# An adaLN block on one core: projections and attention rewritten in front of unchanged experts

## The reference

```
mod = silu(c) @ wmod                            # sa, ca, ga, sb, cb, gb
h = layernorm(x) * (1 + ca) + sa
q, k, v = h @ wq, h @ wk, h @ wv                # 32 query heads, 8 key heads, head width 8
att = softmax(causal(q k^T / sqrt(8)));  y = att @ v @ wo
x = x + ga * y
h = layernorm(x) * (1 + cb) + sb
w = top4_of_2_best_groups(softmax(h @ gate_w))  # 16 experts
x = x + gb * (sum_e w_e * swiglu_e(h) + shared(h))
```

## Time and profile before

| | us |
|---|---|
| median of three runs | 796.46 (795.24 to 807.66) |
| the profiled execution, and its span | 799.05, 797.3 |
| PE, DVE, ACT, POOL busy | 647.6, 456.4, 313.6, 356.1 |
| mean granted TensorE clock | 0.919 of full speed |

### The profile page before, as it was taken

How to read it: one execution, slowest core, us unless ns; L and a number is a source line. 1 busy time by engine, 2 the same in 40 slices (tenths; PEclk the granted TensorE clock), 3 DMA queues, 4 the chain that set the end, 5 groups by cost and what they waited for, 6 DMA issues and landing times.

```text
span 797.3 us, 12982 instructions
## 1 busy us (share of the span) xinstructions
PE 647.6 (81%) x3412; PEld 371.7 (47%) x3412; DVE 456.4 (57%) x751; ACT 313.6 (39%) x673; POOL 356.1 (45%) x440
## 2 busy tenths in 40 slices
PE   1599048999889998999877899992899999999940
PEld 1266023444335444434421555651567777777730
DVE  7576249858786867786728368972133333333317
ACT  1043002757565755575565433320233333333310
POOL 9322302443434352435241145776255666556640
PEclk9999678999999999999995889996899999999985
DMA  6047840315231423232010299656366666666658
GB/s 218 0 143 225 257 145 3 78 30 138 65 99 48 109 79 79 63 94 70 28 29 27 66 370 305 213 190 191 77 104 103 110 109 110 105 103 111 109 74 289
DMA packets 114137, 95.02 MB, mean 119 GB/s; under 512 B 47686, under 2 KB 106022, under 8 KB 114086
## 3 DMA queue, kind: packets, MB, share of 16 engines
q1 hardware_dynamic: 97462, 73.00, 31.8%
q0 software_dynamic: 14448, 19.31, 14.7%
q10 hardware_dynamic: 2176, 2.10, 0.8%
HBM read 47.66 MB, written 44.22 MB: 115 GB/s over the span
## 4 chain that ended last, share of the span: by engine, by line
PE 41%; DVE 11%; DMA 9%; issue 9%; POOL 9%; ACT 5%; SPq 3%; POOLq 0%; DVEq 0%; ACTq 0%
PE bank L980 9%; PE bank L795 7%; PE bank L998 7%; POOL x_rows L1201 6%; DVE negm L1237 5%; PE bank L785 4%; DMA y_sum<-arena 4%; ACT arena L1041 4%; PE bank L767 3%; PE bank L876 3%; DMA arena<-x_rows 3%; PE bank L968 2%; PE bank L813 2%; DVE arena L549 2%; PE bank L989 2%
## 5 line engine op out<-in xcount | busy, mean ns | idle before, releaser
L1041 ACT ACTIVATE arena<-bank 128x512 f32<-128x512 f32 x320 | 176.3, 599 | 117.0 <-PE bank L785 113.2
L1237 DVE TENSOR_REDUCE negm<-bank 128x2 f32<-128x1024 f32 (+3 forms) x176 | 190.8, 1117 | 36.7 <-PE bank L771 35.8
L1208 POOL DMA_INDIRECT y_sum<-arena x79 | 123.0, 1556 | 94.2 <-DVE arena L1455 89.9
L1147 POOL TENSOR_SCALAR_AFFINE_SELECT arena<-arena 128x512 f32<-128x512 f32 x128 | 81.7, 652 | 158.9 <-ACT arena L1041 155.1
L767 PE MATMUL bank<-arena 96*128 96x512 bf16 (+3 forms) x512 | 115.7, 307 | 35.8 <-DVE credits L1223 27.9
L785 PE MATMUL bank<-arena 96*128 96x512 bf16 x320 | 118.7, 399 | 15.8 <-ACT arena L1041 11.2
L980 PE MATMUL bank<-arena 128*128 x316 | 108.8, 467 | 0.3 <-issue 0.3
L771 PE MATMUL bank<-mask_qk,ident_bf 128*128 128x128 bf16 (+2 forms) x352 | 87.8, 250 | 0.0
L795 PE MATMUL bank<-arena 128*32 128x512 f32 x640 | 79.7, 627 | 5.1 <-POOL arena L1147 5.1
L1201 POOL DMA_INDIRECT x_rows<-arena,slots x64 | 63.3, 989 | 45.1 <-DVE slots L1370 26.2
L1448 DVE TENSOR_TENSOR arena<-bank,arena 128x176 f32<-128x176 f32 x79 | 27.0, 341 | 97.4 <-ACT arena L1119 97.4
(11 more groups left out here) (162 smaller groups left out, 750.5 us busy)
## 6 DMA issues: line engine op xcount, KB each, us to landing
arena<-x_rows SPq DMA_DIRECT2D x79, 136.5 KB, 2.5
q_parts<-arena SPq DMA_DIRECT2D x24, 384.0 KB, 3.9
arena<-q_parts SPq DMA_DIRECT2D x32, 288.0 KB
arena<-up_t SPq DMA_DIRECT2D x2, 2816.0 KB, 18.4
arena<-k_parts SPq DMA_DIRECT2D x16, 288.0 KB
y_parts<-arena SPq DMA_DIRECT2D x64, 64.0 KB
arena<-y_parts SPq DMA_DIRECT2D x16, 256.0 KB, 3.2
arena<-y_sum SPq DMA_DIRECT2D x8, 512.0 KB, 6.9
```

The source lines that it names most:

```text
L1041: nc.scalar.activation(pool[:, q % 2, g * QT + kt, :], bank[:, buf, :], ACT.Exp, scale=SCALE).then_inc(s["st_free"], 1)
L1147: nc.gpsimd.affine_select(out=block_, in_=block_, compare_op=ALU.is_ge, fill=0.0, base=0, pattern=[[0, REP], [1, P]], channel_multiplier=- ...
L1208: gp.indirect_dma_start(y_sum[t % 2], bass.IndirectOffsetOnAxis(ap=xt[t % XT][:, D:D + 1].bitcast(U32), axis=0), yo[t % YO], None, compute ...
L1237: nc.vector.tensor_reduce(to, view, AX.X, ALU.max, negate=True).then_inc(s["s_free"], 1)
```

## The change

The experts' code stays. In front of it:

- q parts are stored once (768 KB a batch), k parts too; each half's `Q` and `K` (one `K` now, rows 72 to 74 ones) are loaded whole, in three pieces each, into one of three buffers, two halves ahead.
- V is filled after the first norm, Q not at all, and 32 partitions of each K. Two norms are turned before the first projection, `hT` has two buffers, and q's banks alternate.
- The gates are made once, four batches as four rows, in the middle of the first maxima; SP writes them to memory and loads them broadcast.
- Probabilities stand in 4 slots of one group (4 tiles of one key tile). The diagonal group of a block comes first. PE weighs one group for each group of four exponentials, two groups behind; the eviction of a block comes inside a later group (`LEAVE`).
- The totals leave as one row a head. DVE inverts them as 128 x 64 at group 5; SP stores the inverse and loads it broadcast; the product comes at group 8. The last half inverts as before.
- The halves are unrolled, without loops and the registers of their waits. Statistics of the second norm, shared weights and the zero fills of the experts move ahead.

```diff
-KR = 96
+KR = PR + PARTS
...
+WEIGH = {n: (1, n + 8) if n < 2 else (0, n - 2) for n in range(NG)}
+LEAVE = {1: (1, 3), 2: (0, 0), 4: (0, 1), 7: (0, 2)}
+SLOTS = 4
+QBUF = 3
...
-        pool = take(2, 4 * GH, T)
-        Q = [take(QT, HH, P, dt=BF16) for s in range(2)]
-        K = [take(GH, T, dt=BF16) for s in range(2)]
-        K0 = [take(GH, T, dt=BF16) for s in range(2)]
-        Vc = [take(QT, GH, 32) for s in range(2)]
+        probs = take(SLOTS, GH, T)
+        Q = [take(HH, T, dt=BF16) for i in range(QBUF)]
+        K = [take(GH, T, dt=BF16) for i in (2, 0, 1)]
+        K = [K[1], K[2], K[0]]
...
-                nc.gpsimd.memset(V, 1.0).then_inc(s["v_ones"], 1)
-                for h in range(2):
-                    nc.gpsimd.memset(Q[h][:, :, :, :], 0.0)
-                    nc.gpsimd.memset(K[h][:, :, :], 1.0)
-                    last = nc.gpsimd.memset(K0[h][:, :, :], 0.0)
-                last.then_inc(s["cleared_q"], 1)
...
+                gp.wait_ge(s["xn_ready"], 1)
+                nc.gpsimd.memset(V, 1.0).then_inc(s["v_ones"], 1)
+                gp.wait_ge(s["v_ones"], 1)
+                for i in range(QBUF):
+                    nc.gpsimd.memset(K[i][64:96, :, :], 1.0).then_inc(s["k_ones"], 1)
+                    gp.wait_ge(s["k_ones"], i + 1)
+                low(0)
...
-                    for h in range(2):
-                        for j in range(PARTS):
-                            mine = parts[i][:, h, j, :].unsqueeze(1).to_broadcast([P, PARTS, T])
-                            sp.dma_start(q_parts[b, h, j].rearrange("n d h t -> (d h) n t"), mine).then_inc(q_out[i], 16)
-                        for n in range(PARTS):
-                            sp.dma_start(k_parts[b, h, n].rearrange("j d g t -> (d g) j t"),
-                                         parts[i][32 * h:32 * h + 32, 2, :, :]).then_inc(q_out[i], 16)
...
+                def store_parts(b):
+                    i = b % 2
+                    sp.wait_ge(s["low_done"], b + 1)
+                    sp.dma_start(q_parts[b].rearrange("h j d (n t) -> (d n) (h j) t", n=HH),
+                                 parts[i][:, 0:2, :, :].rearrange("p h j t -> p (h j) t")).then_inc(q_out[i], 16)
+                    sp.dma_start(k_parts[b].rearrange("j h d (g t) -> (h d g) j t", g=GH),
+                                 parts[i][0:64, 2, :, :]).then_inc(q_out[i], 16)
+                def load_half(u):
+                    b, h, i = u // 2, u % 2, u % QBUF
+                    for n in range(PARTS):
+                        rows_ = slice(PARTS * HD * n, PARTS * HD * n + PARTS * HD)
+                        sp.dma_start(Q[i][rows_, :, :].rearrange("p n t -> p (n t)"),
+                                     q_parts[b, h].rearrange("j d m -> (j d) m")).then_inc(q_in[i], 16)
+                        sp.dma_start(K[i][rows_, :, :].rearrange("p g t -> p (g t)"),
+                                     k_parts[b, n, h].unsqueeze(0).to_broadcast([PARTS, HD, GH * T])).then_inc(k_in[i], 16)
...
+                def send_values(u):
+                    h = u % 2
+                    sp.wait_ge(s["o_free"], QT * u + QT)
+                    above(sp, y_in[h], 32 * (u // 2))
                     for g in range(GH):
-                        for k in range(2):
-                            sp.dma_start(y_parts[h, k, g].rearrange("r d t -> d r t"),
-                                         O[h][32 * g + HD * k:32 * g + HD * k + HD, :, :]).then_inc(y_out[h], 16)
...
+                def fetch_values(u):
+                    h = u % 2
+                    sp.wait_ge(y_out[h], 128 * (u // 2 + 1))
...
+                    sp.dma_start(totals, y_totals[h].rearrange("n (a t) -> (n a) t", a=P // (GH * REP))).then_inc(t_in[h], 16)
+                    sp.dma_start(Yp[0][:, :], y_values[h].rearrange("g r d t -> (g r d) t")).then_inc(y_in[h], 16)
+                def spread_inverse(u):
+                    h = u % 2
+                    sp.wait_ge(s["inverted"], u + 1)
+                    sp.dma_start(y_inverse[h].rearrange("n (a t) -> (n a) t", a=P // (GH * REP)), inverse
+                                 ).then_inc(i_out[h], 16)
+                    sp.wait_ge(i_out[h], 16 * (u // 2 + 1))
+                    sp.dma_start(Yp[1][:, :], y_inverse[h].unsqueeze(1).to_broadcast([GH * REP, HD, T])).then_inc(y_in[h], 16)
...
+                store_parts(0)
+                store_parts(1)
+                sp.wait_ge(q_out[0], 32)
+                sp.wait_ge(s["k_ones"], QBUF)
+                load_half(0)
+                load_half(1)
+                store_parts(2)
+                store_parts(3)
+                sp.wait_ge(q_out[1], 32)
+                load_half(2)
+                sp.wait_ge(s["gate_rows"], 1)
+                sp.dma_start(mod_rows, row_mod[0:B, :, :].rearrange("p m d -> p (m d)")).then_inc(s["gate_out"], 16)
+                sp.wait_ge(s["gate_out"], 16)
...
+                for u in range(HALVES):
+                    if u > 0 and u + 2 < HALVES:
+                        sp.wait_ge(s["st_ready"], E_TOT * u)
...
+                        load_half(u + 2)
+                    put_negm(u, QT - 1)
+                    if u > 0:
+                        send_values(u - 1)
+                    if u + 1 < HALVES:
+                        put_negm(u + 1, 0)
+                    if u > 0:
+                        fetch_values(u - 1)
+                    if u + 1 < HALVES:
+                        put_negm(u + 1, 1)
+                    if u > 0:
+                        spread_inverse(u - 1)
+                    if u + 1 < HALVES:
+                        put_negm(u + 1, 2)
...
+                def gate_rows():
+                    pe.wait_ge(s["wg_in"], 16)
+                    for k in range(2):
+                        for c in range(DC):
+                            last = nc.tensor.matmul(bank[0:B, 6 + k, :], sc_sb[:, c, :],
+                                                    wmod_sb[:, c, GA * P + 512 * k:GA * P + 512 * k + 512],
+                                                    start=(c == 0), stop=(c == DC - 1))
+                    last.then_inc(s["gate_mm"], 1)
...
-                def weigh_values(b, h, q):
-                    u = 2 * b + h
-                    pe.wait_ge(s["p_ready"], 16 * u + 4 * q + 4)
-                    pe.wait_ge(s["o_free"], 4 * u + q + 1)
-                    for kt in range(q + 1):
-                        for g in range(GH):
-                            last = nc.tensor.matmul(bank[32 * g:32 * g + 32, OBANK, :], Vc[h][:, kt, g, :],
-                                                    pool[:, q % 2, g * QT + kt, :], start=(kt == 0), stop=(kt == q),
-                                                    skip_group_check=True)
+                def weigh_values(u, n):
+                    b, h, (q, kt) = u // 2, u % 2, GROUPS[n]
+                    pe.wait_ge(s["st_free"], E_TOT * u + GH * n + GH)
+                    if kt == q:
+                        pe.wait_ge(s["p_ready"], GH * (QT * u + q) + GH)
+                        above(pe, s["o_free"], QT * u + q)
+                    for g in range(GH):
+                        last = nc.tensor.matmul(bank[32 * g:32 * g + 32, OBANK, :], V[:, b * QT + kt, h * GH + g, :],
+                                                probs[:, (NG * u + n) % SLOTS, g, :], start=(kt == q),
+                                                stop=(kt == max(q - 1, 0)), skip_group_check=True)
                     last.then_inc(s["av_done"], 1)
...
-                def half(b, h, nxt=True, back=True):
-                    for q in range(QT):
+                def half(u):
+                    for n, (q, kt) in enumerate(GROUPS):
                         for g in range(GH):
-                            ne, ns = q + 1, (s_units(q, g) if nxt else 0)
-                            for k in range(ne):
-                                scores(b, h, q, g, k)
-                                for j in range(k * ns // ne, (k + 1) * ns // ne):
-                                    scores_for_max(b + h, 1 - h, q, g, j)
-                            if g == 1 and q > 0:
-                                weigh_values(b, h, q - 1)
-                            elif g == 1 and back:
-                                weigh_values(*prev(b, h), QT - 1)
-                            if g == 2 and q == 0:
-                                turn_max(b, h, QT - 1, turn_use(b, h, QT - 1))
-                            elif g == 2 and nxt:
-                                turn_max(b + h, 1 - h, q - 1, turn_use(b, h, q - 1))
-                            if h == 0 and back and q == 3 and g >= 2:
-                                project(b - 1, g - 2, project_use(b, g))
+                            slot = GH * (n - FIRST[q]) + g
+                            scores(u, n, g)
+                            if g == 0:
+                                back_, m = WEIGH[n]
+                                if u - back_ >= 0:
```

(64 more changed lines are left out.)

936 lines of the change are left out of this document (428 added, 508 removed).

## The result

The changed kernel takes 764.1 us (median of four runs, 756.5 to 766.2) against 801.5 us for the kernel before on the same chip (four runs, 795.2 to 807.7): ratio 0.954, 95% interval 0.942 to 0.967. Forecast were 711 us and a range of 690 to 742. The direction came as forecast, and so did the time of the first projection and that of the experts; four stages fell short, three of them by much.

A forecast was written before the change was run, and what follows sets the result against it. PE was taken to bound the halves, with waits from bursts of value matmuls; norm fills and repeated q stores the beginning. Terms -52 + 6 - 30.5 - 9 = -85.5 from 797.3 gave 711.8, as a median 711; range 690 to 742.

The forecast's parts named there:

- First norm, first projection: Beginning: first norm set done at 9.2, second held by POOL's fills until 19.5, first projection at 20, 11 us sooner.
- The 17: Beginning: alternative first projection time if DVE gets through after the fill in flight, instead of 20; sum 3 us lower.
- 2.4 MB at 263 GB/s is 9 us, 54 to 55: Beginning: batch 1's stores and the first half's loads finish then; first score at 56 against 108.2, -52 us.
- +6: First maxima: gates now inside, 3.6 us of PE matmuls and 3 to 6 of DVE; bounds 3 to 9.
- that is 30.5, so 5.7 us are waits: Halves: PE's own work in a 36.2 us half is 30.5; waits fall to 2, saving 30.5 us over seven halves.
- Nothing on PE: Halves: the inverse's transfers and six loads ahead of the puts of maxima on SP's queue cost PE no time.
- Waits stay in the halves: Rival, chance 0.16: two score banks, not bursts, make the 5.7 us; 10 saved instead of 30, 731 us.
- The slower rival: Rival, chance 0.03: PE falls to the 1.2 GHz level in the halves; 820 us at 45% of the work.
- The beginning is starved: Rival, chance 0.10: data, not PE, sets the first score at 68; 723 us.
- The inverse: Halves: inverse by store and load costs PE nothing; rival, chance 0.07: late, 3 us in each of seven halves, 732 us.
- Everything flows: Rival, chance 0.09: waits of 0.5 us a half and first score at 50; 692 us.
- Last half: Last half up to the routing: 43.8 falls to 34.9 (31 to 40) through early statistics, -9 us.

The follow-up runs named there:

- e11: e10 with POOL's three fills of K's rows 64 to 96 held until the second batch's normalised rows; 0.920 of the kernel before.
- e2: Changed kernel with each 96 KB K load cut into three loads of 32 KB; 0.935 of the kernel before.
- e7: e2 and e1 together, with the second half's Q and K loads behind the stores of batches 2 and 3; 0.932 of the kernel before.
- e1: Changed kernel with gate matmuls and gate arithmetic moved ahead of the first maxima; 0.947 of the kernel before.
- e9: e7 with the first half's puts of maxima ahead of SP's wait for the gates' store and of the third half's loads; 0.931 of the kernel before.
- e10: e9 with 12 unused filler matmuls on PE ahead of the gates and 10 behind them; 0.929 of the kernel before.
- e5: e2 with values weighed in six bursts of one or two groups a half instead of ten single groups; 0.935 of the kernel before.
- e14: The changed kernel run again, unedited, on one chip with e15 and e16; 0.950 of the kernel before, median 787.8 us.
- e4: Changed kernel with the three zero fills moved from SP's list of the second half to that of the seventh; 0.953 of the kernel before.
- e16: e12 with K loads in the changed kernel's shape, one load per part, in a repeat run; 0.933 of the kernel before, median 771.2 us.
- e15: e12 run again on one chip with the changed kernel; 0.921 of the kernel before, median 761.2 us.
- e12: e11 with the third half's loads, the gates' broadcast load and the shared weights moved later in SP's list; 0.916 of the kernel before.
- e8: e2 and e1 together, with 12 unused filler matmuls on PE ahead of the gates; 0.932 of the kernel before.

## Why the prediction was wrong, step by step

**First norm, first projection: right in the time, in part by luck.** 19.98 us against a forecast of 20, and 6.82 + 1.38 for the first set. The second set took 3.55 us beside three fills, and 1.38 in e11 without them, so that POOL's fills hold DVE is shown. But the forecast had DVE held until the last fill ends and all four instructions behind it, at 19.5. In the trace one instruction gets through after each fill; the set ends at 18.2, and the way from there to the first projection takes 1.8 us where the forecast left 0.5. The Trainium skill (SBUF — State Buffer, "SBUF: two separate sides") says that the ports are locked for one instruction at a time, and the four rows of single fills and instructions above agree with it: each DVE instruction ends with the fill beside it. The 17 that the prediction drew from it let the whole set through after one fill, which is more than that sentence says. The kernel before doesn't agree with it: there one `tensor_scalar` alone took 18.05 us (7.78 to 25.83), through six fills that followed each other without a semaphore wait between them. In the changed kernel POOL waits for each fill before the next, and 0.05 us lie between the two fills shown; that this wait is what lets DVE through was not tested.

```profile
7.78 18.05 DVE L234 TENSOR_SCALAR arena<-X,ln_mv,ln_rs 128x256 f32<-128x256 f32 x1
```

**First score: the step "2.4 MB at 263 GB/s is 9 us, 54 to 55" failed.** It took 22 us from batch 1's low part (44.1) to the first score. Low parts and projections came when they were forecast (35.6 and 44.1 against 36 and 45). Of the 10.5 us missed, the K loads' shape makes 3.5 (e2), the second half's loads issued behind them 3.2 more (e7 against e2: 62.9 to 59.7, where PE's gates have moved too). The other 3.8 stay open; a queue that moved 263 GB/s in stores of 384 KB moved 172 GB/s from 44 to 67 us in this mix of stores and loads. The Trainium skill (DMA: Bandwidth & Descriptors, "Why a DMA increments its semaphore by 16 and not by 1") has a transfer use the largest number of engines, up to 16, that divides the slowest dimensions of both sides, which makes 3 for these loads and 8 for e2's; no run here shows the engines. The prediction had its price, some 3 us, beside the sum and not in it. e2 measured 3.5.

**First maxima: the term "+6" was mis-sized, and a second wait stood behind it.** PE's eight gate matmuls took 5.69 us instead of 3.6, at 1.2 GHz:

```profile
75.54 5.69 PE L541 MATMUL bank<-arena 128*4 128x512 f32 x8
84.89 0.28 PE L592 MATMUL bank<-ident,negm 128*16 128x128 f32 x1 [3.65 <-DVE arena L1152]
```

DVE's nine operations on four partitions took 0.40 each for 256 columns, as bounded, and PE waited 3.65 for them: 9.3 in all, just beyond the upper bound of the term. The remaining 2.5 of the 11.9 I put down to PE at the lower level (granted 0.59 in this stretch), which no run separates. Moving the gates out did not return them (e1), because the puts would have been late behind the gates' round trip and the third half's loads. The prediction costed six loads ahead of a put "at nothing on PE" inside the halves and did not look at the same queue in front of the first half. With gates first and puts first the stretch is 31.5 (e9), with a kept clock at its start 28.5 (e10).

**Halves: 20.6 us short, in three parts.**

(1) An undisturbed half without a projection is 34.1, not 32.5; with two projections 37.6, not 36.5; summed over seven halves 8.8. The step that failed is "that is 30.5, so 5.7 us are waits". From start to start, with PE's idle time taken out, the half from 249.94 of the kernel before and the one from 295.47 of the changed kernel are:

| us of PE | in the sum | before | after |
|---|---|---|---|
| 40 scores | 8.8 | 11.0 | 10.3 |
| scores for the maxima, with masks | 12.3 | 13.6 | 13.2 |
| ten groups of value matmuls | 9.0 | 9.1 | 10.0 |
| turns | 0.4 | 0.4 | 0.4 |
| work | 30.5 | 34.2 | 33.9 |
| idle | 5.7 before, 2 after | 2.0 | 0.2 |

So only 2.0 of the 5.7 were waits, and the earlier trace rows had it: PE busy for 33.97 of 36.00 us. The rest was PE's own work, and it stayed. I had priced each kind by its distance in a dense row of its own; in the changed kernel's mix each costs 7 to 17% more. Why stays open; in e5 the value matmuls in bursts win back 0.6, and the scores lose 0.7.

(2) The second, third and fifth half were held, by 1.3, 6.3 and 0.2 us here: the step "Nothing on PE" for the puts failed. In e14, e1, e4 and e16 the fifth lost 2.8 to 4.3 us too. The step looked at when PE needs the put, 19 us into the half, and that was met: it landed 15 us in. It left out who else waits for the put: POOL's split two later, and behind it in POOL's list the mask. Shown cause of the late landing: the K loads' shape (e2, e15 against e16). The transfers of that put land within 10.7 us here and 10.6 in e16, within 6.7 in e2 and 7.1 in e15. How a load issued 3 us and more ahead holds a put of 12 KB is argued and not shown: the engines with the long loads would be among those that carry the put, which is done when the slowest is. The same section of the Trainium skill says that a transfer of few engines takes the lowest-numbered ones, so that such loads all meet on the same; no run here shows single engines.

(3) The first half lost 4.1 us to PE's 1.2 GHz level at its start, as read from the trace: PE is busy for 38.03 of its 38.26 us, at a granted clock of 0.50 up to 112 us. No experiment took that away; fillers ahead of the first maxima did not.

**"Waits stay in the halves" (731 us)** has the number of its stage, 10 saved against 9.9 measured, by another mechanism. Idle time did go, from 2.0 to 0.2 a half, and seven undisturbed halves would have saved 21.7; the stalls and the clock took 7.8 and 4.1 of it.

**The slower rival** (PE at 1.2 GHz in the halves, 820 us) was the wrong size and not without substance: PE was at that level for most of 66 to 118 us and behind the stalls of the third and the last half. It costs 4.1 us in the first half, and fillers won 3 in the stretch before (e9 to e10). The argument against it, that the clock fell after PE had stood, does not cover all cases: in e15 it fell with PE busy for 74% of the time and no pause over 0.75 us.

**"The beginning is starved" (68, 723 us)** was true of its stage (66.5); the forecast put it at 0.10 because it looked at the bytes and not at their shape and order, which make 6.7 of the 10.5 us missed. **The inverse** was harmless, as said: undisturbed halves have 0.2 us of idle PE. **"Everything flows"** is 692 in the text; its own terms, 1.5 us less in each of seven halves and 6 at the start, give 694.5.

**Last half: 39.3 against 34.9.** Read from the trace, not tested. ACT's root with its two tables takes 2.9 us and PE stands for 2.4 of them, as forecast. Up to that gap ACT paces PE: the other stalls behind it come to 6.3 us in the half, where the sum had 3.4. Behind the gap PE is at the lower level (granted 0.50 from 393 to 400 us), so that two groups of eight value matmuls take 1.94 instead of 1.06, and ACT now waits for PE.

```profile
386.89 1.28 ACT L306 ACT_TABLE_LOAD   x1
...
388.51 1.28 ACT L907 ACT_TABLE_LOAD   x1
...
390.46 1.09 PE L572 MATMUL bank<-arena 75*128 75x512 bf16 x2 [2.41 <-ACT arena L907]
...
396.65 1.94 PE L583 MATMUL bank<-arena 128*32 128x512 f32 x8
```

**Range.** All bad ends together made 745, and 742 was the end stated; three of the four terms were beyond their bad ends (-41.7 at a bound of -42, +11.9 at +9, the halves -9.9 at -14). They were not independent: shape and order of what SP issues have a part in the first score and in the halves, and stood ready behind the gates in the first maxima.

## What to carry to other kernels

Cost a transfer by its place in the queue and by its shape, not by its bytes alone (e2, e9, e12): list for each small, needed transfer what was issued ahead of it on the same queue, and put what nobody needs yet behind it. Ask also who waits for the buffer that it reads. Time that is left over when work is priced from dense rows is not all waiting; compare it with the engine's idle time first. A wait written into a queue's list, here for a store of 16 KB, delays everything behind it by the megabytes ahead of it. When an edit of 9 us returns 2, look in its trace for the wait that took over: e1 shows it (6.73 us for nm_parts), e8 shows where it comes from, and only e9, on top of three edits, takes it away.

## What the runs showed of the hardware

- **The issue of a DMA can block.** Twelve loads of 2.9 MB in all were issued in 8.4 us (45.3 to 53.6), and the next store but one held SP for 14.0 us; its own transfer is 192 KB.
- **The granted clock fell while PE was mostly busy**: 1.00 up to 65 us, 0.50 from 70, between them PE busy for 3.70 of 5 us, and it stayed at 0.50 for 25 us more at shares over 0.9 (e15). In the changed kernel PE was busy for all 12 us from 106 to 118 at 0.50 and 0.56, and was granted 1.00 from 118 to 124.
- **A fill of POOL held the DVE instruction beside it** to 0.15 us after its own end (`tensor_scalar`, fp32, 256 columns: 0.40 alone, 1.02 and 1.98 beside a fill). Where POOL waited between fills, one such instruction passed at each; where it did not, one was held for 18.05 us.
- **Chips differ by one loop.** SP stores 16 pads, each at a row that it first loads into a register. In the runs traced, that takes 20.6 to 20.8 us on the chips where the kernel before has a median of 802 us (its own loop, 20.82, too), and 43.3 to 45.3 on those where it has 826 to 829. The changed kernel on one of each:

```profile
484.43 20.61 SPq L472 DMA_DIRECT2D x_rows<-arena  x16
```

```profile
498.00 44.44 SPq L472 DMA_DIRECT2D x_rows<-arena  x16
```
